# Two sixteen-head attention phases of an eight-phase kernel: compact keys and queries spread by DMA, one run of units over all groups, and the weighting products of two units issued together

## What is computed

```python
x = x + tanh(g_xattn[2]) * _L2_xattn_ref(layernorm(x), ctx, ctx, mask, ...)      # phase 4
x = x + tanh(g_ffn[2])   * _L2_ffn_ref(layernorm(x), ...)                        # phase 5
x = x + tanh(g_xattn[3]) * _L3_xattn_ref(layernorm(x), ctx, ctx, ...)            # phase 6
x = x + tanh(g_ffn[3])   * _L3_ffn_ref(layernorm(x), ...)                        # phase 7

# _L2_xattn_ref, 16 heads of 8 features
scores = einsum('bhqd,bhkd->bhqk', q, k) / sqrt(8)
scores = where(mask == 0, -1e9, scores)
out = einsum('bhqk,bhkd->bhqd', softmax(scores), v)      # heads side by side, then @ Wo.T + bo

# _L3_xattn_ref: no mask; heads 8 to 15 see every second token, their result is upsampled
for i, f in enumerate((1, 2)):
    hs = slice(i * 8, (i + 1) * 8)
    attn = softmax(einsum('bhqd,bhkd->bhqk', Q[:, hs, ::f], K[:, hs, ::f]) / sqrt(8))
    outs.append(upsample_linear(einsum('bhqk,bhkd->bhqd', attn, V[:, hs, ::f]), S))
```

## Time and profile before

| | us |
|---|---|
| median of 3 runs | 1010.61 (1005.93 to 1012.45) |
| the profiled execution | 1011.52, its span 1009.7 |
| PE busy | 907.7 (90%), 4523 products |
| DVE / ACT / POOL busy | 572.8 / 442.1 / 476.4 |
| mean granted clock of TensorE | 0.946 |

### The profile page before, as it was taken

How to read it: one execution, slowest core, us unless ns; L and a number is a source line. 1 busy time by engine, 2 the same in 40 slices (tenths; PEclk the granted TensorE clock), 3 DMA queues, 4 the chain that set the end, 5 groups by cost and what they waited for, 6 DMA issues and landing times.

```text
span 1009.7 us, 13519 instructions
## 1 busy us (share of the span) xinstructions
PE 907.7 (90%) x4523; PEld 602.3 (60%) x4523; DVE 572.8 (57%) x1530; ACT 442.1 (44%) x777; POOL 476.4 (47%) x444
## 2 busy tenths in 40 slices
PE   5989898979899999898989967589899897999998
PEld 5866575656566666464655635355455455666664
DVE  6767454747446643457576556754756645663632
ACT  2334434445252423365656633336455464243321
POOL 3655646466536465535353303332533414756553
PEclk9899999999899999999999977779999997999999
DMA  8202201224032423000000030000000003243141
GB/s 321 84 2 84 74 11 53 84 91 137 31 111 74 132 96 93 0 2 1 2 1 1 1 133 1 0 1 2 1 2 1 1 1 107 82 148 103 71 149 62
DMA packets 32436, 59.28 MB, mean 59 GB/s; under 512 B 4880, under 2 KB 5264, under 8 KB 32112
## 3 DMA queue, kind: packets, MB, share of 16 engines
q1 hardware_dynamic: 32224, 58.42, 17.5%
q10 hardware_dynamic: 144, 0.01, 0.0%
HBM read 56.90 MB, written 1.51 MB: 58 GB/s over the span
## 4 chain that ended last, share of the span: by engine, by line
PE 59%; DVE 7%; ACT 4%; issue 3%; POOL 1%; DVEq 0%; ACTq 0%
PE Y L1040 11%; PE B L868 5%; PE B L870 5%; PE B L869 5%; PE B L1331 5%; PE B L1266 5%; PE B L1346 4%; PE B L1298 4%; PE B L1305 3%; PE B L1297 2%; PE Y L1361 1%; ACT shared L1393 1%; DVE shared_r L1473 1%; PE B L1271 1%; DVE shared_r L1475 1%
## 5 line engine op out<-in xcount | busy, mean ns | idle before, releaser
L1154 POOL TENSOR_TENSOR shared<-shared,bcs 128x512 f32<-128x512 f32 x192 | 245.8, 1283 | 221.2 <-DVE shared L1185 201.2
L1185 DVE TENSOR_TENSOR shared<-shared,B 128x512 f32<-128x512 f32 x204 | 139.4, 686 | 215.0 <-PE B L870 150.8
L1055 ACT ACTIVATE shared<-B 128x512 f32<-128x512 f32 x204 | 121.6, 598 | 284.6 <-PE B L870 284.4
L1040 PE MATMUL Y<-shared,down_lo 128*128 128x512 f32 x408 | 209.9, 602 | 0.0
L1451 POOL TENSOR_TENSOR shared_r<-shared_r,const 128x512 fp32r<-128x512 f32 (+1 forms) x128 | 126.2, 1018 | 141.9 <-DVE shared_r L1475 109.3
L1521 DVE TENSOR_REDUCE mxh<-B 128x4 fp32r<-128x512 f32 (+1 forms) x128 | 79.1, 620 | 63.4 <-PE B L1298 63.0
L1414 ACT ACTIVATE shared<-B 128x512 f32<-128x512 f32 (+1 forms) x128 | 69.7, 544 | 67.2 <-PE B L1305 66.6
L1040 PEld LDWEIGHTS Y<-shared,down_lo 128*128 128x128 f32 x408 | 73.5, 192 | 22.5 <-issue 11.2
L868 PE MATMUL B<-shared_r,gate_hi 128*128 128x512 f32 x102 | 82.8, 812 | 0.0
L868 PE MATMUL B<-x_lo,gate_hi 128*128 128x512 f32 x102 | 76.0, 745 | 0.7 <-ACT shared L1055 0.7
L1331 PE MATMUL B<-const,shared 128*128 128x128 f32 x448 | 73.6, 282 | 0.0
(11 more groups left out here) (288 smaller groups left out, 1719.0 us busy)
## 6 DMA issues: line engine op xcount, KB each, us to landing
bcs<-wrow SPq DMA_DIRECT2D x96, 256.0 KB, 3.6
bcs<-wrow SPq DMA_DIRECT2D x128, 128.0 KB, 3.0
gate_lo<-in_moe SPq DMA_DIRECT2D x9, 256.0 KB, 5.7
up_lo<-in_moe SPq DMA_DIRECT2D x9, 256.0 KB, 6.0
down_lo<-in_moe SPq DMA_DIRECT2D x9, 256.0 KB, 5.8
small<-in_small SPq DMA_DIRECT2D x1, 1378.5 KB, 10.6
X<-in_x SPq DMA_DIRECT2D x4, 256.0 KB, 5.4
CT<-in_ctx_t SPq DMA_DIRECT2D x4, 256.0 KB, 5.7
```

What stands on the lines that cost most here:

```text
L1040: nc.tensor.matmul(Y[:], w_raw[2][:, at:at + P], hid[(n0 + c) % HIDDEN], start=(i == 0), stop=(i == m["NC"] - 1))\
L1055: nc.scalar.activation(sg[(n0 + n) % ACTIVE], B[n % GATES][:], ACT.Silu).then_inc(sem("sg_ready"), 1)
L1154: gp.tensor_tensor(hid[(n0 + n) % HIDDEN], hid[(n0 + n) % HIDDEN], bcs[(PLACE.k0[p] + r // m["PER"]) % BROADCAST], ALU.mult)\
L1185: nc.vector.tensor_tensor(hid[(n0 + n) % HIDDEN], sg[(n0 + n) % ACTIVE], up[:], ALU.mult)\
```

## The change

1. The weights for keys and queries are no longer replicated. PE makes one *compact* product for the keys and one for the queries of a group. ACT adds the bias and writes the upper part (`comp_hi`), DVE the lower (`comp_lo`). SP then copies 32 partitions (one quad) four times, by four DMAs, into `qh[a]` and `kh[a]`: 32 DMAs a group. The layout of 32 partitions a head becomes four copies of 32 partitions a quad; `rowmask` follows.
2. The 64 units of a phase are one run. PE, DVE and ACT iterate `n` = 0 to 72; `t = n % 16` places the compact products, values, next rows, turn-round, result product and finish of neighbouring groups between units, all through bank T. The values get two buffers (`vh`, `vc`), `pt` three.
3. The weighting of units `n-4` and `n-3` stands together in even iterations.
4. In a phase's first quad the four masked keys are made by POOL (one), ACT (one) and DVE (two). The second buffers of the values are set at the program's start by five memsets on POOL.

On PE, the loop over units:

```diff
+            for n in range(NALL + 9):
+                g, t = divmod(n, NU)
+                if n < NALL:
+                    score(n)
+                if 0 <= n - 1 < NALL:
+                    shift(n - 1)
+                if g < NG and t == 0:
+                    next_rows(g)
+                if g + 1 < NG and t == 3:
+                    pe.wait_ge(sem("xhat_t_ready"), s0 + g + 2)
+                    compact(g + 1, "q", T)
+                if g > 0 and t == 6 and p == 6:
+                    upsample(g - 1)
+                if g > 0 and t == 7:
+                    heads_turned(g - 1)
+                if g > 0 and t == 8:
+                    output(g - 1)
...
+                    compact(g + 1, "k", T)
+                if g < NG and t == 11:
+                    result(g)
+                if g + 1 < NG and t == 13:
+                    pe.wait_ge(sem("x_updated"), s0 + g)
+                    values(g + 1, T)
...
+                if 0 <= n - 2 < NALL:
+                    turn(n - 2)
+                if n % 2 == 0:
+                    for u in (n - 4, n - 3):
+                        if 0 <= u < NALL:
+                            weigh(u)
+                for q in (n // GB - 2, n // GB - 3):
+                    if 0 <= q < QUADS * NG and back_at(q) == n:
+                        back(q)
```

On ACT; `high` is called at t == 4 for q and t == 10 for k, and oT's copy stands ahead of the iteration's exp:

```diff
+            def high(g, kq, bank):
+                act.wait_ge(sem("compact_mm"), 2 * (e + g) + "qk".index(kq) + 1)
+                if g:
+                    act.wait_ge(sem(f"heads_{kq}{HEAD_TILES - 1}"), 16 * COPIES * (e + g))
+                nc.scalar.activation(comp_hi[kq][:], bank[:], ACT.Identity, bias=S(f"b{kq}{p}"))\
+                    .then_inc(sem("compact_hi"), 1)
...
+                if g > 0 and t == 7:
+                    act.wait_ge(sem("heads_oT_mm"), e + g)
+                    nc.scalar.copy(oT[:], T[:]).then_inc(sem("heads_oT_ready"), 1)
```

On SP (`query` is alike, waits for the scores of the quad a group earlier, and takes the upper part for c < 2), and in POOL's `each`:

```diff
+            def key(g, a):
+                sp.wait_ge(sem("compact_hi"), 2 * (e + g) + 2)
+                sp.wait_ge(sem("compact_lo"), 2 * (e + g) + 2)
+                if g:
+                    sp.wait_ge(sem("heads_k_each"), eq + QUADS * (g - 1) + a + 1)
+                for c in range(COPIES):
+                    part = comp_hi["k"] if c % 2 == 0 else comp_lo["k"]
+                    sp.dma_start(kh[a][32 * c:32 * (c + 1), :].bitcast(F32), part[32 * a:32 * (a + 1), :].bitcast(F32))\
+                        .then_inc(sem(f"heads_k{a}"), 16)
...
+                pool.wait_ge(sem(f"heads_k{a}"), 16 * COPIES * (e + g + 1))
+                if q >= 2:
+                    pool.wait_ge(sem("heads_score_mm"), eu + GB * (q - 1))
+                for i in (0,) if q == 0 else range(HEAD_TILES):
```

On DVE, behind each unit's maximum:

```diff
+                if g + 1 < NG:
+                    if t == 4:
+                        low(g + 1, "q", T)
+                    if t == 10:
+                        low(g + 1, "k", T)
+                    if t == 14:
+                        values(g + 1, T)
...
+                    if t == 12:
+                        finish_dve(dve, (g + NG - 1) % NG, s0 + g)
+                    if t == 8 and g < NG - 1:
+                        norm_stats(st, (g + 2) % NG)
+                    if t == 14 and g < NG - 1:
+                        apply(s0 + g + 2, (0, 1))
+                    if t == 15 and g < NG - 1:
+                        apply(s0 + g + 2, (2, 3))
+                if p == 6:
+                    if n == NALL - 8:
+                        x_low_dve(dve, 7)
+                    if n == NALL:
+                        pieces = route_dve(dve, st, 7)
+                    next(pieces, None)
```

More of the change, by code:

```diff
@@ L537, in setup_dve @@
                 st.add(v.tensor_tensor(ybias[:, p:p + 1], bcols[:, k:k + 1], tgate[:, p:p + 1], ALU.mult))
-            for p in (4, 6):
-                for k in range(2):
-                    st.add(v.tensor_scalar(b_low[p][:, k, :], S(f"b{'qk'[k]}{p}"), K("low")[:, k:k + 1], None, ALU.mult))
             yield
@@ L1454, in heads_pool, with power @@
                 ins.then_inc(sem("heads_k_each"), 1)
+            def power(s):
+                pool.wait_ge(sem("var_ready"), s + 1)
+                nc.gpsimd.tensor_tensor(rstd[:], var[:], minus_half[:], ALU.pow).then_inc(sem("rstd_ready"), 1)
+            power(s0 + 1)
+            each(0, 0)
+            each(0, 1)
+            for g in range(NG):
+                each(g, 2)
+                each(g, 3)
+                if g + 1 < NG:
+                    power(s0 + g + 2)
+                    each(g + 1, 0)
+                    each(g + 1, 1)
@@ L1540, in build @@
+            for _ in pieces:
+                pass
         area5 = Area()
@@ L1806, in _ @@
                 elif p > 3:
[L1807 to L1811 removed]
+                    heads_pool(pool, p)
         @block.scalar
```

596 lines of the change are left out of this document (310 added, 286 removed).

## The result

| kernel | median us | ratio to before, 95% interval |
|---|---|---|
| before | 1011.5 (1005.9 to 1012.5, 4 runs) | |
| changed | 984.9 (983.4 to 986.1, 4 runs) | 0.9747 [0.9708, 0.9786] |

What follows compares the result with a forecast made beforehand. TensorE (PE), busy 90% of the span, was taken as the bound, with a loop through the exp as long. -23.8 - 29.6 - 7.3 + 1 + 2.6 + 1 = -56.1 from 1011.5 gave 955 us; range 940 to 980.

Steps and rivals of the forecast that it cites:

- (a): Phases 4 and 6: weighting two units together makes a pair 3.38 us for 3.12 in phase 4, 0.26 worse.
- (b): 64 units as one run: first to last score 127.1 us for 150.9 in phase 4, 117.7 for 147.3 in phase 6.
- VectorE late before a maximum: A term of phase 6's score run in (b): 0.5 us, three times.
- bank T chains the engines: Rival: nine hand-overs a group through one bank make engines wait, +36 us, to 991; chance 0.12.
- (c): Spreading by SP's DMAs: keys hidden in phase 4, 0.8 us late in phase 6; first groups' queueing +1.
- ACT's wait in the first group: At iteration 4 of each phase's first group, ACT waits for query copies: +0.5 us each, 4 at slow pace.
- 0.8 late, 2.0 at the upper bound: Phase 6 group transitions: masked keys for score 16 come 0.8 us late, 2.0 at the upper bound.
- The slow copies: Rival: SP's copies issue 0.64 us apart and land after 3.0, adding 16 us, to 971; chance 0.13.
- (d): Before first scores: phase 4 gains 3.2 us, phase 6 4.1; together -7.3, to -3 at the slow bounds.
- Half clock: Half-speed first units add 1.3 us a phase, +2.6; half clock inside a phase would show the prediction wrong.
- The forecast's test for late keys: PE waiting over 2 us for GpSimd's masked keys at unit 16, 32 or 48 would show the prediction wrong.
- (e): Phase 6's last group: one more routing step ahead of VectorE's L1504, sigmoid's table load behind the last copy: +1 us.

Runs made afterwards that it cites:

- e13: e10 with GpSimd waiting, in the prologue, for VectorE's next normalised rows before quad 1's key products; 949.4 us.
- e1: Changed kernel with VectorE writing the next group's normalised rows in iterations 11 and 12 instead of 14 and 15; 976.4 us.
- e9: Changed kernel with both edits: keys before queries, and VectorE's normalised rows in iterations 11 and 12; 951.4 us.
- e7: Changed kernel with the same instructions reordered: keys projected and copied before queries; 964.2 us.
- e2: Changed kernel with one 128-partition copy per quad instead of four of 32, so the output is not the reference's; 969.9 us.
- e14: e13 with six idle products added in each prologue; 945.7 us.
- e4: Changed kernel with nine idle 512-column products added in each of the two prologues; 985.8 us.
- e10: e9 with quad 1's four key copies, in each phase's first group, issued by ACT's queue instead of SP's; 954.3 us.

## Why the prediction was wrong

- **(a) Pairing: right.** 1.78/1.53 for 1.83/1.56 in phase 4; 1.64/1.40 (fine, e13's first group) and 1.40/1.24 for 1.73/1.33 and 1.43/1.16 in phase 6. Alternation as described. (32 x 1.83 + 31 x 1.56 is 106.9, not 106.8.)
- **(b) One run: right in mechanism but for iteration 0; that the sum then fits is in part luck.** With the late hand-overs gone (e13) the spans are 126.3 and 116.2 where this step gave 127.1 and 117.7, the latter with 2.4 for late keys that e13 doesn't have. But e13's four groups of phase 4 are 30.2, 33.3, 33.3 and 29.6 us long, and this step's terms, laid out by group, make 32.8, 32.4, 32.4 and 29.5. The start-up, put at 3.0, cost 0.3, with the clock at half speed at its beginning. A middle group cost 0.9 more than forecast: 0.4 in iteration 0, 0.3 at the turned outputs (3.83 for 3.54), and 0.5 in iteration 11, whose finish was to fit the idle time and took 2.10 for 1.56; bare iterations gave some of it back. The two errors have opposite signs.
- **The step that failed in (b): VectorE's next rows cost nothing.** I charged PE's four transposes of them (0.44), counted VectorE's time as cover, and never asked what runs on GpSimd in the same microseconds. Before, VectorE's rows and GpSimd's products stood apart. Now `apply` stands in iterations 14 and 15, where GpSimd's eight products (8.02 us) run. It is not in the list of rivals ("VectorE late before a maximum", 1.5 in phase 6, is another place); "bank T chains the engines" came nearest, with 991 us, but the bank is not what holds them up. Price: e1 against the changed kernel 8.4 us (5.8 against its repetition) in phase 4, e9 against e7 another 6.3 in phase 6.
- **(c) Copies: mechanism right, sizes off, and one wait misplaced.** This is the second step that failed: the pace of SP's queue. I took 0.47 and it was 0.63; the landing 2.3 and it was 2.0. ACT's wait in the first group was "+0.5 each" at the fast pace and 4 at the slow; it was 3.1 and 3.7, and iterations 5 to 8 of the first groups took 10.4 more than forecast. The keys in phase 6 were "0.8 late, 2.0 at the upper bound": 1.2 to 1.9 more than in the kernels where they are in time. The slow copies had a chance of 0.13 at 971, and their pace was what the rows of the last burst showed; a burst of six from another place outweighed it in my choice. By e7 the copies' lateness and order were worth 18.5 us in the changed stages, more than the rival's 16. Behind the waits the clock fell as well (phase 6's granted clock is 0.88 in the changed kernel and 0.92 in e7); how much of the gain is the clock's no run separates.
- **(d) Prologues: -5.3 for -7.3.** First scores came 10.9 and 11.9 us into the phases (9.7, 11 forecast). With one copy for four (e2) they came at 7.7 and 10.3: again the number of issues and their pace.
- **Half clock.** "Half clock inside a phase" was named as what would be wrong, and it came: the granted clock is 0.93 and 0.88 in the two runs, 1.00 in e14. It follows the waits. What the start alone costs was put at 2.6 and measured 2.0 (e14), and 3.0 in iterations 0 to 3 by themselves.
- The forecast's test for late keys, a wait of over 2 us at units 16, 32 and 48, was too coarse: it was met once in six (2.12 at unit 48 of phase 6). Three more waits of 0.65 to 1.68 us, and two for the rows alone in phase 4, were enough, with the clock falling behind some of them.
- **(e) Ends: +2.9 for +1; the step was named and priced too low.** It isn't chance: the rest after the last score is 182.4 us in both profiles of the kernel before and 185.1 to 186.7 in those of all other kernels. In the changed kernel 2.2 us of it stand before phase 6's last result product, which starts 13.6 us after the last score where it started 11.4 after it. The routing step that now goes ahead of VectorE's division (L1615) waits for ACT's sigmoid, and PE's way back waits 3.11 us for that division, where it waited 0.47 for ACT. VectorE, then PE:

```profile
803.65 0.29 DVE L656 TENSOR_TENSOR s<-sig,small 128x128 f32<-128x128 f32 x1 [3.67 <-ACT sig L901]
...
805.53 0.41 PE L1343 MATMUL Y<-const,shared 128*128 128x128 f32 x2 [3.11 <-DVE shared L1615]
```

## What to carry to other kernels

When work moves into the shadow of other work, list for each microsecond what all engines do there, not only the one that bounds: VectorE's cheap operations between two SBUF tiles are not cheap beside a run of GpSimd's. Of two tiles that are needed at the same time, send the one with more steps behind it first. A queue of many small copies has a price per copy; price it by the slower of the bursts seen, and look for the buffer that an engine can't overwrite until the last of them has landed. And a fix that only moves a wait (e4, e10) is no sign that the wait was free: the same edits paid once the next wait was gone (e14, e13).

## What the runs showed of the hardware

- VectorE's `TENSOR_SCALAR` from SBUF to SBUF takes 0.34 us for 128x128 with GpSimd idle and up to 1.06 to 1.08 beside GpSimd's products (e10), which last 1.04: each ends just behind the end of one product. 128x512 takes 0.47 alone (e13) and 1.26 to 1.37 beside them; GpSimd's then stretch from 1.04 to 1.22 (e10). VectorE's maximum from PSUM stays at 0.68 to 0.69, beside them too. The Trainium skill's page "SBUF — State Buffer", section "Who interferes with whom", says that the two engines share a port pair as an exclusive lock held for a whole instruction, that `tensor_scalar` can take it and `tensor_reduce` on Trainium2 never does; the traces agree with each of these. Read against the iteration in which `apply` stands, this rule would have foreseen the late rows; it says nothing of the late copies.
- Copies within SBUF leave SP's queue 0.63 us apart when they have 32 partitions and 0.65 apart with 128 (e2), and land 2.0 and 2.4 us after their issue. All four are medians; single copies took longer.
- Two executions of one kernel put TensorE's half-speed stretches in other places outside the changed phases: phases 0 to 3 began phase 4 at 408.8 and 414.9 us, and phase 5's stage took 86.2 and 92.7.
